# Two tiles of keys weighed in one burst: four bursts an iteration instead of eight

## The reference

```
q, k, v = split(x @ W_qkv.T)                  # 16 heads of width 16, 1024 tokens in each of 4 batches
attn = where(causal, (q k^T) / 4, -inf)       # 1024 x 1024 a head
attn = softmax(attn)
y = attn @ v
```

## Time and profile before

| | |
|---|---|
| median of three runs | 2163.37 us (2162.11 to 2169.87) |
| the profiled execution | 2173.41 us, of which the span of the trace is 2171.7 us |
| attention phase in the trace | about 433 to 933 us, its 16 iterations from 461 us on |
| TensorE busy, share of the span | 2039.2 us, 94% |
| VectorE, ScalarE, GpSimd busy | 1474.9 us, 1019.5 us, 922.9 us |

### The profile page before, as it was taken

One profiled execution on the slowest core, in us unless ns is written; L12 is line 12 of the kernel. 1 busy time (PEld: TensorE's weight loads), 2 busy tenths in 40 slices (PEclk: granted clock), 3 DMA queues, 4 the chain that ended last, 5 costly groups with the idle time before them and its releaser, 6 DMA issues.

```text
span 2171.7 us, 41820 instructions
## 1 busy us (share of the span) xinstructions
PE 2039.2 (94%) x13717; PEld 1420.4 (65%) x13717; DVE 1474.9 (68%) x4020; ACT 1019.5 (47%) x2367; POOL 922.9 (42%) x1139
## 2 busy tenths in 40 slices
PE   6999999899999999978999998999989999799998
PEld 5899995434444444357899995666666666566676
DVE  5343655388888888534387658989866666588884
ACT  4433334336666666733434343333346666533332
POOL 5323655321111111114323555555556666455553
PEclk9999999979999999996999999999999999999999
DMA  6556654544443344012555652000000000000000
GB/s 188 190 193 207 240 192 129 151 56 60 60 60 48 49 54 60 2 43 93 176 194 200 226 185 51 0 0 0 1 1 2 2 2 2 2 11 19 10 20 20
DMA packets 101711, 173.58 MB, mean 80 GB/s; under 512 B 14705, under 2 KB 66321, under 8 KB 101521
## 3 DMA queue, kind: packets, MB, share of 16 engines
q1 hardware_dynamic: 95376, 154.40, 27.1%
q0 software_dynamic: 6144, 16.79, 2.4%
HBM read 136.01 MB, written 34.87 MB: 79 GB/s over the span
## 4 chain that ended last, share of the span: by engine, by line
PE 35%; DVE 11%; issue 5%; ACT 3%; POOL 2%; DVEq 0%; DMA 0%; POOLq 0%; ACTq 0%; SPq 0%
PE s_HH L788 5%; PE s_Y L800 5%; PE s_Y L1854 4%; PE s_HH L1824 3%; PE s_R L1824 3%; PE s_HH L2176 3%; PE s_R L455 2%; PE s_R L2163 1%; PE s_R L2197 1%; DVE ff_hscale L1537 1%; PE s_R L2211 1%; PE s_Y L2247 1%; PE s_Y L2255 1%; DVE fw_down L1540 1%; DVE s_HH L1717 1%
## 5 line engine op out<-in xcount | busy, mean ns | idle before, releaser
L1432 DVE TENSOR_REDUCE a_part_max<-a_psS 128x1 f32<-128x512 f32 (+3 forms) x608 | 362.4, 654 | 76.2 <-PE a_psS L1360 67.6
L1488 ACT ACTIVATE a_PT<-a_psE 128x512 f32<-128x512 f32 (+1 forms) x608 | 309.2, 584 | 175.8 <-PE a_psE L1376 158.9
L1335 POOL TENSOR_SCALAR_AFFINE_SELECT a_PT<-a_PT 128x512 f32<-128x512 f32 x128 | 81.2, 635 | 398.9 <-ACT a_PT L1488 398.9
L1767 POOL TENSOR_TENSOR fw_down<-fw_down,ff_hm 128x704 f32<-128x704 f32 x64 | 97.3, 1520 | 249.7 <-DVE fw_down L1549 249.7
L1854 PE MATMUL s_Y<-w_down,fw_up 128*128 128x256 f32 x768 | 181.0, 386 | 22.6 <-ACT fw_up L1804 20.9
L1789 ACT ACTIVATE ff_hm<-fw_down 128x704 bf16<-128x704 f32 x64 | 50.6, 790 | 280.5 <-DVE fw_down L1540 280.5
L1854 PEld LDWEIGHTS s_Y<-w_down,fw_up 128*128 128x128 f32 x768 | 143.5, 191 | 47.8 <-ACT fw_up L1804 30.7
L1824 PE MATMUL s_R<-w_gate,ff_xqT 128*128 128x512 f32 (+1 forms) x512 | 163.8, 463 | 4.8 <-ACT ff_sil L1799 4.8
L1824 PE MATMUL s_HH<-w_up,ff_xqT 128*128 128x512 f32 (+1 forms) x512 | 162.5, 460 | 3.6 <-DVE fw_down L1540 2.4
L1392 PE MATMUL a_psO<-a_PT,a_va 128*32 128x512 f32 (+3 forms) x1536 | 150.4, 494 | 2.5 <-POOL a_PT L1335 1.8
L1354 PE MATMUL a_psS<-a_sk,a_sq 96*128 96x512 bf16 (+2 forms) x480 | 143.7, 334 | 1.9 <-DVE a_part_max L1432 0.3
(11 more groups left out here) (484 smaller groups left out, 4335.2 us busy)
## 6 DMA issues: line engine op xcount, KB each, us to landing
e_w<-w_in SPq DMA_DIRECT2D x70, 1024.0 KB, 5.1
e_xs<-sorted_x SPq DMA_DIRECT2D x70, 128.0 KB
e_xr<-sorted_x SPq DMA_DIRECT2D x70, 128.0 KB, 4.3
sorted_y<-e_yo SPq DMA_DIRECT2D x70, 128.0 KB
a_sq<-qk_parts SPq DMA_DIRECT2D x60, 128.0 KB, 6.4
a_sk<-qk_parts SPq DMA_DIRECT2D x60, 128.0 KB, 6.9
sq<-qk_parts SPq DMA_DIRECT2D x36, 128.0 KB, 5.9
sk<-qk_parts SPq DMA_DIRECT2D x36, 128.0 KB, 6.4
```

What stands on the lines that cost most here:

```text
L1335: pool.affine_select(out=hidden, in_=hidden, compare_op=ALU.is_ge, fill=0.0, base=0, pattern=[[0, HG], [1, P]], channel_multiplier=-1).the ...
L1432: dve.tensor_reduce(part_max[:, c, h0:h0 + heads, qt], psS[place % RING][:, 0:heads * n].rearrange("p (h k) -> p h k", h=heads), AX.X, ALU ...
L1488: act.activation(PT[kt % 2][:, h0:h0 + heads, q0:q0 + n], psE[e % RING][:, 0:heads * n].rearrange("p (h q) -> p h q", h=heads), ACT.Exp, s ...
L1767: c.link(pool.tensor_tensor(hv[i], hv[i], hm[i][:], ALU.subtract))
```

## The change

The loop over key tiles in `order` goes by twos: both tiles of a pair are weighed when the second one is due. The bursts stand at steps 18 (kt 0 and 1), 29 (2 and 3), 37 (4 and 5) and at step 2 of the following iteration (6 and 7). So that the weights of the first tile of a pair can stay, `PT` has four buffers; buffer i holds keys tile i or i + 4 and is 1024 - 128 i queries wide, and a helper `weights` takes the offset into account. `exps` waits for the burst four tiles back instead of two. The number and the shapes of the matmuls, reduces and exponents are unchanged.

```diff
+    WEIGHTS = 4
...
-            for kt in range(BT):
-                due = last_e[kt] + LAG
+            for kt in range(0, BT, 2):
+                due = last_e[kt + 1] + LAG
                 if due < E and j == due and it < ITS:
                     yield "weigh", it, kt
+                    yield "weigh", it, kt + 1
                 elif due >= E and j == due - E and it > 0:
                     yield "weigh", it - 1, kt
+                    yield "weigh", it - 1, kt + 1
...
-        PT = [sb(f"PT{i}", [P, HG, SEQ]) for i in (0, 1)]
+        PT = [sb(f"PT{i}", [P, HG, SEQ - i * P]) for i in range(WEIGHTS)]
...
+        def weights(kt, heads, q0, q1):
+
+            first = kt % WEIGHTS * P
+            return PT[kt % WEIGHTS][:, heads, q0 - first:q1 - first]
...
-                                       PT[kt % 2][:, h, q0:(c + 1) * 512], start=kt == 0,
+                                       weights(kt, h, q0, (c + 1) * 512), start=kt == 0,
...
-                if kt >= 2:
-                    act.wait_ge(weighted, it * BT + kt - 1)
+                if kt >= WEIGHTS:
+                    act.wait_ge(weighted, it * BT + kt - WEIGHTS + 1)
                 elif it > 0:
-                    act.wait_ge(weighted, (it - 1) * BT + (HALF if c == 0 else BT) - 1 + kt)
-                act.activation(PT[kt % 2][:, h0:h0 + heads, q0:q0 + n],
+                    act.wait_ge(weighted, (it - 1) * BT + (0 if c == 0 else WEIGHTS) + kt + 1)
+                act.activation(weights(kt, slice(h0, h0 + heads), q0, q0 + n),
```

More of the change, by code:

```diff
@@ L1333, in _ @@
                     pool.wait_ge(e_drained, it * E + last_diagonal[kt] + 1)
-                    hidden = PT[kt % 2][:, :, kt * P:(kt + 1) * P]
+                    hidden = weights(kt, slice(0, HG), kt * P, (kt + 1) * P)
                     pool.affine_select(out=hidden, in_=hidden, compare_op=ALU.is_ge, fill=0.0, base=0,
```

## The result

The changed kernel takes 2176.47 us (2168.77 to 2181.80 over 20 runs), the kernel before in the same rounds 2169.98 us (2161.13 to 2174.16, 20 runs). The ratio is 1.0038 with a 95% interval of 1.0024 to 1.0053: slower by 0.38%, about 8 us; the two medians differ by 6.5 us and the two means by 7.8. The prediction had +2.7 us and no change that could be told. The sign of the sum was right; its size, and with it the outcome, was wrong. Of the 10.5 us between the forecast median of 2166 and 2176.47, 6.6 come from the kernel before, whose median was 2163.37 in the first three of its runs and is 2169.98 over all 20.

The account below looks back on a forecast made before the run. TensorE and VectorE, through the s ring, were taken to limit alternately. Terms 0.47 + 0.22 - 0.25 - 0.25 an iteration gave +3.3 us, less 0.6 at the end: +2.7, median 2166; own range 2160 to 2172, whole range 2150 to 2178.

Parts of the forecast that it names:

- The mechanism: Attention iterations: pairing saves switches, but longer bursts empty VectorE's ring and ring waits grow; net 0.19 us more an iteration.
- Steps 19 to 29: To the end of the pair 2 and 3: VectorE limits, 8.13 us becomes 8.35, 0.22 more.
- The last iteration: No s pieces, ScalarE's pace: +0.9 or 1.0 from early pairs, last burst ends 1.6 us sooner; together -0.6 us.
- The last but one: Iteration before the last: counted with the early stretches' losses, without the two late savings of 0.25 us each.
- Switch of mode, 0.25 a burst: TensorE bursts: entering costs 0.10 us and leaving 0.15, and half of the 128 bursts lose it.
- The joint costs nothing: Between two key tiles back to back in a double burst: nothing taken, so tiles 0 and 1 last 3.35 us.
- third rival: The 0.25 us belongs to each key tile, so the joint costs it again; 17 us more at most, 2180; chance 0.05.
- Four buffers cost nothing: PT buffers elsewhere in SBUF: exponents and clearing keep their shapes, so nothing, with 0 to 0.02 us a piece as ends.
- Steps 3 to 18: To the end of tile 1's burst: VectorE idles once for longer, 12.39 us becomes 12.86, 0.47 more.
- Steps 30 to 37: After the pair 2 and 3: TensorE limits at the end, so the switch is saved, 0.25 us less.
- 0 to 2: Pair 6 and 7, two bursts and three pieces: nothing held up, 0.25 us less.
- second rival: VectorE limits all four stretches: 1.13 us more an iteration, +16 us, 2180; chance 0.10.

Follow-up runs that it names:

- late pairs: Kernel before with four PT buffers and only key tiles 4 and 5, and 6 and 7 paired; 2164.95 us, ratio 0.9983 to the kernel before.
- light maxima: Each maximum read only the first 64 keys per head, in the kernel before and the changed kernel; iterations of 28.26 and 27.29 us.
- the two repeats: Second and third profiles of the changed kernel, nothing altered; 2172.47 and 2174.20 us.
- pairs in all iterations but the last, pairs but last: Changed kernel, but with eight single bursts in the last iteration; 2173.55 us, ratio 1.0028 to the kernel before.
- the first eight experiments: four buffers, late pairs, early pairs, pairs but last, light before, light after, wait early, split late; the kernel before took 2168.22 (29 runs) and 2168.47 (11).
- light after: Changed kernel with maxima over only the first 64 keys of each head in a piece; 2129.3 us, ratio 0.9815 to the kernel before.
- early pairs: Kernel before with four PT buffers and only key tiles 0 and 1, and 2 and 3 paired; 2182.36 us, ratio 1.0069 to the kernel before.
- four buffers: Eight single bursts at the steps of the kernel before, but with the four PT buffers; 2167.04 us, ratio 1.000 to the kernel before.
- light before: Kernel before with maxima over only the first 64 keys of each head in a piece; 2138.08 us, ratio 0.9862 to the kernel before.
- wait early: Changed kernel with the wait for loads moved from the s piece of step 29 to the e piece of step 28; 2169.19 us, one run.
- split late: Kernel before with four PT buffers, tiles 4 to 7 paired and tile 0 halved at steps 8 and 13; 2150.59 us, ratio 0.9914 to before.
- split only: Kernel before with four PT buffers and only tile 0 halved, at steps 8 and 13; 2157.54 us, ratio 0.9961 to the kernel before.

## Why the prediction was right and wrong, step by step

The mechanism held, and three terms of the sum were mis-sized. Steps 19 to 29 were put at +0.22 us and took +0.32, in 14 iterations. The last iteration was put at -0.6 and took +0.66, because TensorE's clock fell in it. The last but one was put at +0.2 and took -0.60, which hid part of the other two. The phase thus grew by 4.9 us in place of 2.7. What lies outside the phase was put at nothing, and the timed means differ by 2.5 us more than the phase does.

**Switch of mode, 0.25 a burst.** Right. It is seen by itself in four places: -0.23 and -0.24 for the two late pairs, -0.47 for both in the kernel with late pairs, -0.97 for all four with light maxima.

**The joint costs nothing** (third rival). Right: 3.35 us by the rows, not 3.6.

**Four buffers cost nothing.** Right: 29.66 and a ratio of 1.000; at the end of the phase they save 0.8 us by themselves, 0.2 of the -0.60 and 0.6 of the last iteration's saving below.

**Steps 3 to 18, +0.47.** Right to the hundredth: 12.86. **Steps 30 to 37 and 0 to 2, -0.25 each.** Right, -0.23 and -0.24, so the second rival falls: VectorE is not the limit there.

**Steps 19 to 29, +0.22.** Mis-sized: +0.32. I let the s piece of step 29 start at 5.31 us after the double burst and the burst after 0.54 more; it started at 691.09 - 685.68 = 5.41. The instruction carries a second wait, for its loads. The prediction does not mention it and so had it at nothing; the loads had landed some 7 us earlier. With that wait elsewhere, the step is 0.31 behind its e piece and not 0.40. Counted over the 14 full iterations, 0.10 each, it is 1.4 us of the miss.

**The last but one iteration, counted as +0.22.** Wrong sign: -0.60. I gave it the cost of steps 19 to 29 and neither of the last two savings. It has s pieces only up to step 28: the pair 2 and 3 costs 0.13 there (from the end of tile 1, 7.69 us before, 7.82 after), and from there to the end of tile 7 the pairs save 0.73 (7.35 and 6.62).

**The last iteration, -0.6.** The term was right for the full clock and wrong for the clock it got. Without the fall it is 0.66 - 1.36 = -0.70. The pair at half the clock gives 1.36 us back in this profile, 1.99 and 1.39 in the two repeats. No row of before could show it, since the clock there is full: the single bursts start every three to five us. But the prediction held that this iteration runs at ScalarE's pace, the merge puts its e pieces in a longer row without a burst, and it did not ask what the clock does then.

The sum of the phase: 4.91 us in the profile compared, as 4.85 - 0.60 + 0.66. The prediction's 2.7 is 3.1 + 0.2 - 0.6 in the same parts. The first part is missed by 1.7 (1.4 of it by steps 19 to 29, the rest by hundredths in the late pairs), the second by 0.8 the other way, the last by 1.3.

**From the phase to the run.** In the rounds of the change the medians differ by 6.5 us, the means by 7.8, and the ratio's interval is about 5 to 11 us; the phase explains 5.3. The rest, 2.5 us of the means, lies outside the phase, where no instruction is changed. There the granted clock differs from run to run. Over 126 us from about the end of the phase, before and in the profile with pairs in all iterations but the last:

```profile
934.00:1060.00 126.00, 103.70 (x574) 90.15 (x575) 48.75 (x245) 47.63 (x125) 37.32 (x38) 0.80 0.26 89
```

```profile
934.00:1060.00 126.00, 100.69 (x646) 87.94 (x640) 53.51 (x267) 50.33 (x135) 43.41 (x47) 0.92 0.31 103
```

The same program text gets 0.80 in one and 0.92 in the other. Over the 40 timed runs of before in the rounds of the first eight experiments a mean clock lower by 0.001 goes with a time longer by 1.7 us, over the 20 of after by 1.4. After had 0.9748 on the mean and those 40 runs of before 0.9767; the clocks of before in the rounds of the change itself are not on record. About half of that difference is the fall in the last iteration: 3.4, 6.8 and 3.4 us at half the clock in the three profiles are 0.0010 of the mean clock, and the phase counts them already. The other 0.0009 is worth some 1.3 us, so that about 1 us stays unassigned, which the interval allows. Runs of the same mean clock, 0.979, agree with the phase: 2169.8 us for after (4 runs) and 2164.3 for before (7 runs in the rounds of all experiments), 5.5 apart.

The kernel with late pairs gains 4.9 us on the mean and 8.9 by its phase. Its clock is lower by 0.0019 with no fall in the phase, which is worth some 3 of the missing 4.0. For light after the two measures differ by 3.2 us, for the other kernels with several timed runs by 1.5 at most. Why some kernels draw a lower mean clock stays open, and the profiles do not show where. In the 126 us after the phase they have 0.78, 0.86 and 0.85 for after and 0.80 for late pairs, against 0.80 twice for before. I made no run that sets it.

**The chances.** With steps 19 to 29 and the clock put right the sum would have been near +5, at 0.23% still within the 0.5% that I took for what a measurement can tell. It told 0.38%, from 20 runs of each. The outcome was missed by that as much as by the terms: a bound of 0.5% was too wide for 20 runs of each kernel, and a loss that is computed on each of 15 iterations deserved more than 0.15 for slower. The measured 2176.47 lies outside the forecast's own 2160 to 2172 and inside the whole range of 2150 to 2178, which was drawn wide for the rivals, and none of them came true: that it holds the time is luck.

## What to carry to other kernels

Joining long bursts on one engine saves the switch only where the burst is shorter than the work that the other engine has left in its ring; past that, the slower engine stands still. Here VectorE had 1.15 us of reduces left when the burst of tile 1 began. So compute, for each stretch, which engine is the limit between bursts. Where it is the other one, cut the bursts to about what it has left (here 1 us of burst), and join them where it is not. The pace of VectorE and the length of the bursts were varied here, the ring's depth was not, so for other rings this is an inference. At the ends of a phase, where the producer's work has run out, ask what the clock does when long bursts alternate with thin work.

## What the runs showed of the hardware

- TensorE's granted clock fell to 0.50 although by its records the engine never stood still for longer than 0.3 us since its last burst. In the 4.1 to 6.6 us between that burst's end and the fall it made only e pieces, in some of these stretches also the turn of an output; a piece of 512 columns is 0.22 us of work, and the starts lie 0.49 us apart in the regular part and 0.64 at most. The clock fell so in the last iteration in 3 of 3 profiles of the changed kernel, in that of early pairs and twice in that of light maxima with four bursts. It did not within the phase of before (two profiles), four buffers, late pairs, pairs but last, light before, wait early, split late and split only, once the first iterations are past. The kernel with the wait moved has the same bursts and 4.8 us of the same e pieces after its double burst, and no fall, so it does not come with the order alone. The Trainium skill, TensorE: Matmul & The Clock Gate, section "HAM oscillation — how this bites in real kernels", gives the absence of idle gaps of TensorE as the rule that keeps the clock; here there was no gap of that kind and the clock fell, so against that rule the measurement decides. Part 1 of the same page has the clock follow how busy TensorE has been of late, and with that the e pieces before the fall agree. What the fall costs is 1.2 to 2.0 us a burst (3.71 in place of 2.51 with early pairs, 5.34 in place of 3.35 in the first repeat).
- A second semaphore wait on a matmul that is on the path costs 0.07 to 0.09 us, even where that semaphore has long been reached (29.99 against 29.92 an iteration, 0.40 against 0.31 to the s piece, one profile).
- The two halves of the change add to the hundredth: -0.47 and +0.79 make 0.32, and 0.32 was measured. For a pipeline that two engines limit in turn, stretches can be computed one by one from distances between starts.
